# Waiting tile by tile instead of step by step in front of GpSimd's gathers in a graph layer

## The reference

```python
Q, K, V = (einsum('nc,rch->rnh', x, W) + b for W, b in ((Wq, bq), (Wk, bk), (Wv, bv)))  # per relation
score = sum(Q[type, dst] * K[type, src], -1) / 8          # per edge and head
seg = dst * 5 + type                                       # softmax over the edges of one (node, relation)
e = exp(score - segment_max(score, seg)[seg])
alpha = e / segment_sum(e, seg)[seg]
out = segment_sum(V[type, src] * alpha, dst)               # per node
return layernorm(x + out + bias)
```

## Time and profile before

| | us |
|---|---|
| three timed runs | 2263.09, 2265.75, 2269.71 |
| median | 2265.75 |
| the profiled execution | 2287.36 |
| its span, from the first instruction to the last | 2285.5 |
| GpSimd busy | 1180.8 |
| gathers of the edge stage (831 of L543) | 811.3 |
| VectorE busy | 1566.4 |
| TensorE matmuls busy | 1686.4 |
| ScalarE busy | 1056.2 |

### The profile page before, as it was taken

One profiled execution on the slowest core, in us unless ns is written; L12 is line 12 of the kernel. 1 busy time (PEld: TensorE's weight loads), 2 busy tenths in 40 slices (PEclk: granted clock), 3 DMA queues, 4 the chain that ended last, 5 costly groups with the idle time before them and its releaser, 6 DMA issues.

```text
span 2285.5 us, 33477 instructions
## 1 busy us (share of the span) xinstructions
PE 1686.4 (74%) x7580; PEld 1156.2 (51%) x7597; DVE 1566.4 (69%) x3882; ACT 1056.2 (46%) x4084; POOL 1180.8 (52%) x1261
## 2 busy tenths in 40 slices
PE   8999994227999994476667676667776667676778
PEld 4555541003444442355556555556665556565667
DVE  8888983002433442587878888878888878888877
ACT  3333320001000000057767776767776767777775
POOL 3111127763666204656666666666666666666514
PEclk9999997658999996699999999999999999999998
DMA  8988737765999737888888888888888888888733
GB/s 231 276 237 232 211 117 240 226 195 200 320 332 331 253 151 235 259 274 262 285 277 275 276 284 276 277 284 276 274 277 282 278 280 281 266 280 275 247 114 113
DMA packets 346899, 574.72 MB, mean 251 GB/s; under 512 B 45265, under 2 KB 239985, under 8 KB 346702
## 3 DMA queue, kind: packets, MB, share of 16 engines
q0 software_dynamic: 87920, 276.07, 39.9%
q1 hardware_dynamic: 225770, 235.79, 31.4%
q10 hardware_dynamic: 33012, 60.73, 7.2%
HBM read 411.99 MB, written 140.96 MB: 242 GB/s over the span
## 4 chain that ended last, share of the span: by engine, by line
PE 31%; POOL 26%; issue 23%; DVE 11%; another core or an unknown queue 6%; ACT 2%; DMA 1%; SPq 0%; DVEq 0%; ACTq 0%; POOLq 0%
POOL region L543 26%; PE sums L715 20%; PE sums L784 4%; PE pairs L795 3%; DVE region L1110 3%; DVE region L1311 1%; PE sums L842 1%; PE sums L853 1%; ACT region L982 1%; DVE region L1234 1%; DVE region L1235 1%; DVE region L1236 0%; ACT acc L1000 0%; DVE region L1368 0%
## 5 line engine op out<-in xcount | busy, mean ns | idle before, releaser
L543 POOL DMA_INDIRECT region<-kv_tab,kvidx x831 | 811.3, 976 | 582.6 <-issue 196.6
L715 PE MATMUL sums<-region,acc 128*128 128x512 f32 (+2 forms) x1568 | 676.5, 583 | 7.5 <-ACT acc L867 4.9
L982 ACT ACTIVATE region<-region 128x64 f32<-128x64 f32 x2392 | 662.2, 346 | 0.9
L795 PE MATMUL pairs<-region 128*128 128x256 f32 x1664 | 433.3, 405 | 204.9 <-DVE region L1311 115.9
L784 PE MATMUL sums<-region 128*128 128x131 f32 x3328 | 459.2, 293 | 150.6 <-issue 144.5
L784 PEld LDWEIGHTS sums<-region 128*128 128x128 f32 x3328 | 427.7, 203 | 209.1 <-issue 196.3
L715 PEld LDWEIGHTS sums<-region,acc 128*128 128x128 f32 (+1 forms) x1568 | 297.0, 194 | 308.3 <-issue 284.7
L795 PEld LDWEIGHTS pairs<-region 128*128 128x128 f32 x1664 | 316.5, 200 | 268.2 <-issue 227.3
L1279 DVE TENSOR_TENSOR region<-sums,region 128x512 f32<-128x512 f32 (+1 forms) x215 | 146.4, 690 | 373.7 <-PE sums L715 163.2
L525 POOL DMA_INDIRECT region<-q_tab,region x288 | 273.6, 950 | 156.1 <-issue 81.8
L1000 ACT COPY acc<-sums 128x256 f32 x832 | 303.7, 365 | 96.6 <-remote 51.6
(11 more groups left out here) (244 smaller groups left out, 969.3 us busy)
## 6 DMA issues: line engine op xcount, KB each, us to landing
region<-q_seg SPq DMA_DIRECT2D x832, 128.0 KB
kv_tab<-region ACTq DMA_DIRECT2D x42, 1280.0 KB
q_seg<-region SPq DMA_DIRECT2D x288, 128.0 KB
q_tab<-region SPq DMA_DIRECT2D x48, 640.0 KB, 4.2
region<-rel_tab SPq DMA_DIRECT2D x208, 128.0 KB
region<-region POOLq DMA_DIRECT2D x47, 384.0 KB, 5.5
region<-kv_tab,kvidx POOLq DMA_INDIRECT x831
region<-in_x SPq DMA_DIRECT2D x96, 128.0 KB, 3.1
```

Source lines behind the costliest of these rows:

```text
L543: pool.indirect_dma_start(ring_row[:, a:a + 2 * C], None, kv_tab, bass.IndirectOffsetOnAxis(ap=kvidx[:, t:t + 1], axis=0)).then_inc(s_got[ ...
L715: done = nc.tensor.matmul(bank[o % 4][0:n, 0:w], acc[:, k, t * P:t * P + n], w_sb[:, k, :, :].rearrange("p u c -> p (u c)")[:, c0:c0 + w], ...
L795: done = nc.tensor.matmul(qk[:, i, :], oht[:, s % 2, i * P:(i + 1) * P], qring[:, s % QS, i, :], start=True, stop=True)
L982: done = nc.scalar.activation(ring_v[:, i, spot(q), h * D:(h + 1) * D], ring_v[:, i, spot(q), h * D:(h + 1) * D], ACT.Copy, scale=alT[:, h ...
```

## The change

GpSimd no longer waits, ahead of a step's first gather, until all four tiles of step s - 18 are summed. In front of each gather it now waits until the tile whose place that gather overwrites is summed: i + 1 tiles of that step for tile i, or i + 2 where the key falls into the next tile's row. The wait for the product of step s - 5 stays ahead of the first gather. All other engines keep their programs.

```diff
             for s in range(NSB):
-                if s >= KS - KL:
-
-                    pool.wait_ge(s_agg, SB * (s - KS + KL + 1))
                 if s >= KL:
 
                     pool.wait_ge(s_mul, s - KL + 1)
@@
                     if t >= USED:
                         continue
+                    if s >= KS - KL:
+
+                        done = i + 2 if spot(s) == KS - 1 else i + 1
+                        pool.wait_ge(s_agg, SB * (s - KS + KL) + min(done, SB))
                     a = (i * KS + spot(s)) * C
                     pool.indirect_dma_start(ring_row[:, a:a + 2 * C], None, kv_tab,
```

## The result

The changed kernel takes 2314.97 us (median of 4 runs, 2311.84 to 2320.94), the kernel before on the same chip 2267.73 us. The ratio is 1.0214, with an interval from 1.0195 to 1.0234: 47 us slower. The forecast was 2246 us, faster; 2314.97 also lies outside the range.

What follows compares the result with a forecast made beforehand. GpSimd's gather rhythm was taken as the bound: four gathers at 1.40 us plus a 0.53 us stop. Five gathers per stop saves 20 us: 2287.36 to 2267 profiled, scaled to 2246 us; range 2232 to 2255, 8 in 10 2196 to 2312.

Steps and rivals of the forecast that it cites:

- what bounds the step: Edge stage: GpSimd's own rhythm of four gathers and one stop sets the step, 6.13 us predicted against 6.16 measured.
- the 1.40 us per gather instruction: GpSimd's gathers: behind each lies about 1.40 us of work, more than the 1.25 us in which the next is issued.
- the added waits at 0: In front of the later gathers of a step: the three new waits cost 0 us; at most 125 us.
- all come out when it has drained: TensorE's signals: most are held while gather work is outstanding, and all come out once it has drained.
- once the tiles that got through are used up, the next gather waits for a held signal, and gets it when the longer run has drained: GpSimd's stop moves from the head of a step to a gather inside it, costing the fixed 0.53 us.
- five gathers per stop at 0.53 us each: GpSimd's edge stage: 5 gathers between stops instead of 4, saving 0.11 us a step, 20 us in all.
- if runs of more than 4 gathers starve the other engines: Stated condition under which the prediction is wrong, beside a stop costing other than 0.53 us.
- the third rival: The rival "the early gather shuts the door": ScalarE copies later, next sums wait for copied columns; slower, chance 0.26.
- the early gather shuts the door: Gathers let go early delay signals of tiles 2, 3 and lift; GpSimd stops more often: 2316 to 2366 us, chance 0.26.
- Prompt signals: TensorE's signals are prompt and every head wait was real; saving limited to about 101 us, 2166 us; chance 0.07.
- Nothing changes: Runs settle at 4 gathers with the stop at another tile, or VectorE sets the step: 2266 us, chance 0.26.

Runs made afterwards that it cites:

- waits of both kernels: Changed kernel with the wait for all four tiles put back before the first gather, the three new waits kept: 2283.88 us, ratio 1.0011 to the kernel before.
- three first: Changed kernel, but the first gather of a step waits for three tiles instead of one: 2359.95 us, ratio 1.0340 to the kernel before.
- two first: Changed kernel, but the first gather of a step waits for two tiles instead of one: 2370.66 us, ratio 1.0395 to the kernel before.
- runs of three: Kernel before, but one wait in front of every third gather, for all tiles these three overwrite: 2366.87 us, ratio 1.0443.
- runs of five: Kernel before, but one wait in front of every fifth gather, for all tiles these five overwrite: 2376.15 us, ratio 1.0500.
- four from tile 2: Kernel before, but its one wait per four gathers stands before tile 2 instead of tile 0, for the tiles these overwrite: 2313.53 us, ratio 1.0202.
- tile 2, last of four: Kernel before, but the one wait stands before tile 2 and asks for all four sums of the later step: 2270.63 us, ratio 1.0020.
- tile 3, last of four: Kernel before, but the one wait stands before tile 3 and asks for all four sums of the later step: 2262.54 us, ratio 0.9986.
- tile 1, last of four: Kernel before, but the one wait stands before tile 1 and asks for all four sums of the later step: 2284.46 us, ratio 1.0077.

## Why the prediction was wrong

*Right:* what bounds the step, the 1.40 us per gather instruction (a ratio of about 1.50 expected and 1.504 measured for twice the gathers; 10.10 and 10.11 us for a run of seven), and the added waits at 0 (1.0011 with both kinds of wait). Too strong was "all come out when it has drained". In the run of 28 gathers from which it was read, the product of step 0 had started 0.11 us after its lift's recorded end, some ten gathers into the run (from the views of the earlier trace rows):

```profile
884.94 3.75 PE L795 MATMUL pairs<-region 128*128 128x256 f32 x8 [14.24 <-DMA region<-q_seg]
...
888.80 1.22 DVE L1311 TENSOR_TENSOR region<-region,pairs 128x1024 f32<-128x1024 f32 x1 [2.59 <-issue]
```

*Wrong:* the step "once the tiles that got through are used up, the next gather waits for a held signal, and gets it when the longer run has drained", with five gathers per stop at 0.53 us each. It took the price of a stop for a constant, and every signal that GpSimd would wait for to be a held one; some were for sums not yet made. The average price can be read from each trace: 180 steps' time less 720 x 1.40 us of gather work, over the stops in them.

| kernel | stops in 180 steps | us a step | us per stop | ratio |
|---|---|---|---|---|
| before | 179 | 6.163 | 0.57 | 1 |
| waits of both kernels | 179 | 6.149 | 0.55 | 1.001 |
| changed | 194 | 6.345 | 0.69 | 1.021 |
| three first | 157 | 6.548 | 1.09 | 1.034 |
| two first | 184 | 6.600 | 0.98 | 1.040 |
| runs of three | 149 | 6.630 | 1.24 | 1.044 |
| runs of five | 139 | 6.617 | 1.32 | 1.050 |
| four from tile 2 | 155 | 6.351 | 0.87 | 1.020 |
| tile 2, last of four | 175 | 6.090 | 0.50 | 1.002 |
| tile 3, last of four | 179 | 6.061 | 0.46 | 0.999 |
| tile 1, last of four | 171 | 6.168 | 0.60 | 1.008 |

The steps are from one execution each, on chips that differ by up to 1%, so the first decimal of the price is what counts. That a profile is slower by some 20 us is no rule (tile 2, last of four: 2261.03 us profiled, a median of 2270.63). The 21.6 us of the kernel before, spread over 208 steps, would be 0.10 us of its step (an estimate), so 0.57 may well be 0.47. Runs of five did exactly what the prediction wanted, five gathers per stop and 40 stops fewer, and have the highest ratio of the table: a stop costs more than double on average. In the changed kernel there are 3.7 gathers per stop and not 5. The 15 stops more cost 15 x 0.57 = 8.5 us and the higher price 194 x 0.125 = 24 us, together the 33 us that the two profiles differ by in these steps. The rest of the 47 us isn't located; the profile of the kernel before, being above its median, hides some of it.

The average hides two kinds of stop, as the runs of five show best. Those that start at tiles 0, 1 and 2 (25, 25 and 34 of them) take 7.46, 7.50 and 7.48 us on average, as predicted (5 x 1.40 + 0.53 is 7.53). The 34 that start at tile 3 take 10.21 us, and the stop behind them is 4.14 us long. One of these:

```profile
1444.43 0.94 POOL L549 DMA_INDIRECT region<-kv_tab,kvidx  x1 [1.22 <-remote]
...
1445.61 1.96 PE L790 MATMUL sums<-region 128*128 128x131 f32 x16
...
1451.63 0.27 ACT L979 COPY region<-bank 128x128 f32<-128x128 f32 x1 [4.54 <-remote]
...
1453.90 0.36 ACT L1006 COPY acc<-sums 128x256 f32 x1
...
1454.43 2.03 PE L790 MATMUL sums<-region 128*128 128x131 f32 x16 [3.40 <-issue]
...
1455.87 0.94 POOL L549 DMA_INDIRECT region<-kv_tab,kvidx  x1 [5.49 <-PE sums L790]
```

This run starts when all four sums of a burst are known, so "part of a burst" is not the whole reason. The next burst is made during the run, from 1445.61; ScalarE idles for 4.54 us until the five gathers are worked off (1.40 x 5 + 0.30 after 1444.43 is 1451.73) and makes the last copy at 1453.90. Only then does TensorE begin, at 1454.43, the burst whose first sum GpSimd asks for. So a stop keeps its price where the sum asked for is made by the time the run is worked off. It is dear where TensorE can begin that burst only after copies that the run itself held up; the runs of eight from tile 2 end in the same way (copy at 1670.19, burst at 1670.74). GpSimd then waits for sums being made, which in the changed kernel the chain shows (TensorE's sums and lift on 26.9%). A sentence of the prediction named this as what would make it wrong ("if runs of more than 4 gathers starve the other engines"), and its own row spoke for it: behind long runs the product idles for 15.33 and 7.89 us. I set that aside because ScalarE needs only 2.2 us for three late copies. That TensorE's next sums wait for those copies stands in the third rival, but the forecast gave that wait no price.

*The rival* "the early gather shuts the door" had the mechanism, copies held longer (172.9 us for 83.2) and sums that wait for them. That it also had the time (2316) is in part luck: its price was for 267 stops in 178 steps at 0.53; there were 195, and dearer. *Prompt signals* would have needed hardly any gap over 0.5 us. *Nothing changes* failed with the ratio. That TensorE's clock is the cause was not tested apart; in the timelines of the changed kernel and of the runs of four it falls after TensorE has idled, and with the last of four asked for it is 0.97 in the even stretch, as good as the 0.96 of before.

The Trainium skill's "TensorE: Matmul & The Clock Gate" (The cost: per-tile semaphore tail) has about 26 ns per signal. By that, as an estimate, a burst's four signals would be out some 0.1 us after it. This trace does not agree: the news came 3.25 us after the recorded end of its burst (1377.49 to 1380.74).

What stays open is which part of the chip holds TensorE's signals while gathers are outstanding; the runs show only for how long. Nor do they show why some signals come through at once, or why a stop in the unchanged rhythm costs 0.5 us and not less. Runs of five that ask for a whole burst each time were not tried.

## What to carry to other kernels

A coarse wait can do a second job: here the wait for the last of four sums made sure that all news of a burst was out before the next work went in front of it. Before a wait is split or brought forward, look at who else waits for the same signals and what the earlier work will put in front of them. Asking for the last signal is not enough by itself: the next stop must not ask for work that can begin only after news which the run holds up. And a stop has a price beside its number: read both from the trace, since fewer stops at a doubled price are a loss.

## What the runs showed of the hardware

- An indirect gather on GpSimd holds signals of TensorE for about 1.40 us per instruction, with 128 rows or 64 (a step of four takes 6.16 and 6.24 us), with 512 numbers a row or 256 (6.16 and 6.18 us); eight gathers of half the columns take 11.60 us a step. Over a run of 28 the news came after 34.49 to 39.57 us, 39.50 being the full sum.
- The hold ends before the data is signalled as landed: 5.94 against 9.09 us after the first of four gathers.
- Some signals do come through during a run (the copies at 1662.69 and 1663.43 above); it is these that let GpSimd skip a stop.
